# Products that nobody reads in TensorE's waits, and three first-pass products moved into the last projection

## The chip, the cores and the metric

One core of a Trainium2 chip runs the whole program in one launch. The metric is device time in microseconds (us), as a median over runs. TensorE multiplies matrices, VectorE (DVE) and ScalarE (ACT) work on rows of elements, GpSimd (POOL) does the same more slowly, and SyncE (SP) issues the transfers to and from memory. TensorE has two clock levels, 1.2 and 2.4 GHz; the profile lists which share of the full one was granted.

## The reference, cut to what matters

A half-weighted feed-forward layer with eight gated experts, an attention layer and the same feed-forward layer again, each on a layer-normalised input and added to x. x has 4 x 1024 rows of 128 elements.

```python
x = x + 0.5 * _L0_ffn_ref(_layernorm(x), ...)
x = x + _L0_attn_ref(_layernorm(x), ...)
x = x + 0.5 * _L0_ffn_ref(_layernorm(x), ...)
...
# attention: 16 query heads of 8 elements, 4 key/value heads
q = (qkv @ Wq + bq).reshape(B, S, H, dh).transpose(0, 2, 1, 3)
...
scores = jnp.einsum('bhgqd,bhkd->bhgqk', qg, k) * scale
bias = slopes.reshape(KVH, G, 1, 1) * rel
bias = jnp.where(causal, bias, -jnp.inf)
attn = jax.nn.softmax(scores + bias[None], axis=-1)
out = jnp.einsum('bhgqk,bhkd->bhgqd', attn, v)
```

## The kernel before, in words

The 4096 rows are cut into 8 groups of 512 (`GROUPS`, index `c`). The first feed-forward layer is done for all groups; its last stage, `ffn_down`, does for each group the down products (`down`), and on the way the layer norm, the transposition (`xn_T`) and the projections to queries, keys and values for attention (`project`). A projection is one product for the queries (`wq`, 512 columns), four for the values and four for the keys. ACT takes queries and keys out of PSUM (`qk`: `qp`, `qf`, then `kp`, `kf`), DVE and POOL split them into three bfloat16 parts, SP stores the parts to memory (`store_parts`) and loads them back in the layout that attention reads (`load_stack`).

Attention runs over 16 units (a batch entry and a key head). It has two passes. The first finds the maximum of each query's scores: TensorE makes 38 products per unit (`piece`, numbered by `n`), and DVE reduces each one from PSUM (`reduce`). The products of the next unit are made while the second pass of the current one runs (`score`, the exponential on ACT, `times_v`). A ring of three PSUM banks (`RING`) holds the first-pass products: product n can be made only when the one three places before it in the ring has been reduced. The second pass needs the maxima as rows beside the queries; DVE computes them (`maxima`), TensorE transposes them (`maxima_T`), DVE copies them out (`rows_out`, tile `wt`), and SP transfers them (`load_maxima`).

Unit 0 has no unit before it. Its first-pass products start inside `ffn_down`: products 0 to 18 are spread over groups 4 to 7 by `EARLY`, six more (19 to 24, `TAIL`) stand around the transposition of group 7, ahead of its projection, and the last 13 stand at the start of attention. Everything is ordered by hand: each engine runs its list in the written order, and a wait holds up all that stands behind it on that engine.

Three lists matter here.

- TensorE: products 12 and 13, transposition of group 6, products 14 and 15, projection of group 6, products 16 to 18, `maxima_T(0, 0)`, products 19 to 21, transposition of group 7, products 22 to 24, projection of group 7, products 25 to 37, then `score`.
- DVE: reductions 19 to 24, `values(7)` (takes the values of group 7 out of PSUM; it waits until ACT has written `kf`), reductions 25 to 27, `middle(7)` (the second part of group 7's queries, placed by `LAST_SPLIT`), reductions 28 to 37, `maxima(0, 1)`.
- SP: `load_maxima(0, 0, 0)`, `store_parts(7)` (waits until POOL has made the last parts, which wait for `middle(7)`), a wait until all stores have landed, then `load_maxima(0, 0, 1)`. `score` of step 4 of unit 0 waits for that last load (`a_wd[1]`).

Of the kernel before, what the change touches and what calls it, by code (L numbers as in the profile page):

```python
# [2 lines left out]

# [14 lines left out]
GROUPS = TILES // GT  # L18
# [91 lines left out]

EARLY_END = sum(map(sum, EARLY))
TAIL = (3, 3)
LAST_SPLIT = EARLY_END + sum(TAIL) + 3
assert FIRST_HALF <= early(GROUPS - 1, 1).start and LAST_SPLIT < NP1
W1_STEP = 0
# [14 lines left out]
def after(eng, sem, value):  # L131

    if value > 0:
        eng.wait_ge(sem, value)
# [42 lines left out]
def macaron(nc, dram, out):  # L177
    ctx = ExitStack()
    with ctx:
# [17 lines left out]
        c128 = sb("c128", [P, 8 * P])  # L197
# [135 lines left out]
        def bank(b):  # L333
            return ps[:, b, :]
# [723 lines left out]
        def _(pe):  # L1058
            def mm(o, l, r, start=True, stop=True):
                return pe.matmul(o, l, r, start=start, stop=stop, skip_group_check=True)  # L1060
# [59 lines left out]
                    up(k)  # L1120

            def ffn_down(f, qkv):
                def early_pieces(some):
                    for n in some:
                        if n == 0:
                            pe.wait_ge(a_ld[0][0], 16 * LOADS)
                            pe.wait_ge(s_ks0, 4)
                        if n == SECOND_STACK:
                            pe.wait_ge(a_ld[1][0], 16 * LOADS)
                        piece(0, n)  # L1130

                def down(c, par, transpose=False):
                    pe.wait_ge(f.hm, MASK_PARTS * (c + 1))
                    after(pe, f.x, c - 1)
                    if c == 1:
                        pe.wait_ge(f.h, len(TILE_ORDER))
                    for t in range(GT):
                        if transpose and t == GT // 2:
                            xn_T(c - 2)
                        if transpose and t == GT - 1:  # L1140
                            early_pieces(early(c - 1, 0))
                        rows = slice(t * P, (t + 1) * P)
                        for i in range(HT):
                            ins = mm(ps[:, y_bank(qkv, par), rows], h_all[:, c, i, rows], wds[:, i, :],
                                     start=(i == 0), stop=(i == HT - 1))
                    ins.then_inc(f.Y, 1)

                def project(c, par):
                    pe.wait_ge(f.xTb, c + 1)
                    after(pe, f.qf, c)  # L1150
                    mm(bank(5), wq[:, :], xnT[:, par, :]).then_inc(f.Q, 1)
                    w = KVH * DH
                    after(pe, f.v, c)
                    for t in range(GT):
                        ins = mm(ps[:, 4, w * t:w * t + w], xnT[:, par, t * P:(t + 1) * P], wkv[:, w:2 * w])
                    ins.then_inc(f.V, 1)
                    after(pe, f.kf, c)
                    for t in range(GT):
                        ins = mm(ps[w * t:w * t + w, 4, P:2 * P], wkv[:, 0:w], xnT[:, par, t * P:(t + 1) * P])
                    ins.then_inc(f.K, 1)  # L1160

                def xn_T(c):
                    pe.wait_ge(f.xn2, c + 1)
                    after(pe, f.xTb, c)
                    turn(lambda t: xn[:, t, :], 3).then_inc(f.Tb, 1)

                def body(c, par, first, last):
                    if not last:
                        down(c + 1, 1 - par, qkv and not first)
                    if qkv and last:  # L1170
                        xn_T(c - 1)
                        early_pieces(early(c, 0))
                    if qkv and not first:
                        project(c - 1, 1 - par)
                        early_pieces(early(c, 1))

                pe.wait_ge(f.wds, 1)
                down(0, 0)
                over_groups(body)
                if qkv:  # L1180
                    maxima_T(0, 0)
                    early_pieces(range(EARLY_END, EARLY_END + TAIL[0]))
                    xn_T(GROUPS - 1)
                    early_pieces(range(EARLY_END + TAIL[0], EARLY_END + sum(TAIL)))
                    project(GROUPS - 1, 1)

            ring = Ring()

# [69 lines left out]
            def attention():  # L1258
                def next_stack(i, par, half):

                    pe.wait_ge(a_ld[half][1 - par], 8 * LOADS * (i + 3 if par else i + 2))

                pe.wait_ge(a_ld[1][0], 16 * LOADS)
                for n in range(EARLY_END + sum(TAIL), NP1):
                    piece(0, n)
                pe.wait_ge(a_wd[0], 32)
                for p in range(SLOTS):
                    score(0, 0, p, 0)

                def body(i, par, first, last):  # L1270
                    def pieces(s, k):
                        for n in () if last else part(s, k):
                            if n == 0:
                                next_stack(i, par, 0)
                            if n == SECOND_STACK:
                                next_stack(i, par, 1)
                            piece(i + 1, n)

                    for s in range(NSTEP):
                        pieces(s, 0)  # L1280
                        if s + 1 == QT:
                            pe.wait_ge(a_wd[1], 32 * (i + 1))
                        if s + 1 == NSTEP and not last:
                            pe.wait_ge(a_wd[0], 32 * (i + 2))
                        for p in range(SLOTS):
                            if s + 1 < NSTEP:
                                score(i, s + 1, p, par)
                            elif not last:
                                score(i + 1, 0, p, 1 - par)
                            pieces(s, 1 + p)  # L1290
                        if s >= LAG:
                            times_v(i, s - LAG, par)
                        elif not first:
                            times_v(i - 1, NSTEP + s - LAG, 1 - par)
                        pieces(s, 3)
                        if s == W1_STEP:
                            maxima_T(i, 1)
                        if s == OT1_STEP and not first:
                            out_T(i - 1, 1)
                        if s == OT0_STEP:  # L1300
                            out_T(i, 0)
                        if s == W0_STEP and not last:
                            maxima_T(i + 1, 0)

                over_units(body)
                for s in range(NSTEP - LAG, NSTEP):
                    times_v(UNITS - 1, s, 1)
                out_T(UNITS - 1, 1)
# [92 lines left out]
```

## Time and profile before

| | us |
|---|---|
| median of 3 runs (lowest to highest) | 728.12 (727.83 to 728.29) |
| the profiled execution's own time | 728.65 |
| its span, first to last instruction | 726.8 |
| mean granted TensorE clock | 0.977 |

| engine | busy us | share of the span |
|---|---|---|
| TensorE products (PE) | 699.3 | 96% |
| TensorE weight loads (PEld) | 364.1 | 50% |
| DVE | 567.9 | 78% |
| ACT | 406.6 | 56% |
| POOL | 139.6 | 19% |

The page cuts the span into 40 slices of 18.2 us and gives the busy share of each engine in tenths, and the granted clock. The chain that ended last is the work that set the end, followed back from the last instruction; TensorE has 59% of it and DVE 16%. Most of the span is attention, whose 16 units repeat a period of 25.7 us. The change is at its head, between about 148 and 186 us.

### The profile page before, as it was taken

The page shows a single profiled execution, that of the slowest core. Times are in us where ns is not written, and L with a number is a line of the kernel's source. Part 1 is how long each engine was busy: PE and PEld are TensorE (multiplying, and loading weights), DVE is VectorE, ACT ScalarE, POOL GpSimd, SP SyncE. Part 2 cuts the span into 40 slices and gives each one's busy share as a digit, 9 for nine tenths or more (in the row PEclk, how much of TensorE's full clock was granted, in tenths as well). Part 3 has the DMA queues.
Part 4 walks back from the last instruction along what each step waited for, and adds up shares of the span by engine and source line. Part 5 has one row for each costly group of instructions (what it writes and reads, how often), then busy time and mean ns, then how long its engine had stood idle before and what let it go on. Part 6 is the DMA issues. An engine that isn't in the chain of part 4 may idle for free.

```text
span 726.8 us, 15935 instructions
## 1 busy us (share of the span) xinstructions
PE 699.3 (96%) x5906; PEld 364.1 (50%) x5906; DVE 567.9 (78%) x1880; ACT 406.6 (56%) x587; POOL 139.6 (19%) x157
## 2 busy tenths in 40 slices
PE   8999999979999999999999999999999789999998
PEld 4554498833344444444444444444444265544597
DVE  6976338697999999999999999999999148775311
ACT  3353353224776777777777677777767843353200
POOL 3202895552000000000000000000000002104950
PEclk9999999965999999999999999999999999999999
DMA  8014533443001001100100110010010000005651
GB/s 221 1 17 75 92 70 115 142 150 105 21 21 39 21 22 38 39 21 21 39 21 21 39 31 25 24 39 21 21 40 1 2 1 1 1 1 100 107 87 59
DMA packets 47249, 34.69 MB, mean 48 GB/s; under 512 B 13106, under 2 KB 46514, under 8 KB 47172
## 3 DMA queue, kind: packets, MB, share of 16 engines
q1 hardware_dynamic: 46596, 33.60, 19.3%
q8 instruction: 47, 0.77, 0.5%
q14 instruction: 30, 0.25, 0.1%
q10 hardware_dynamic: 576, 0.08, 0.1%
HBM read 23.01 MB, written 10.39 MB: 46 GB/s over the span
## 4 chain that ended last, share of the span: by engine, by line
PE 59%; DVE 16%; issue 13%; DMA 4%; SPq 3%; POOL 3%; ACT 2%; DVEq 0%; ACTq 0%; POOLq 0%
PE ps L1060 55%; DVE mx L945 8%; PE ps L1065 4%; POOL h_all L495 2%; DMA mask_second<-sel_scr 2%; DVE mx L938 1%; ACT h_all L653 1%; DMA yT<-sel_scr 1%; DVE xn L734 1%; DMA k_scr<-kp 1%; SPq L392 1%; DVE stats L722 1%; DVE h_all L938 1%; SPq L389 1%; DVE wb L965 1%
## 5 line engine op out<-in xcount | busy, mean ns | idle before, releaser
L653 ACT ACTIVATE h_all<-ps 128x1024 f32<-128x1024 f32 (+3 forms) x384 | 291.3, 810 | 108.3 <-PE ps L1060 105.2
L945 DVE TENSOR_REDUCE mx<-ps 128x1 f32<-128x512 f32 (+2 forms) x352 | 223.0, 681 | 9.5 <-PE ps L1060 6.5
L1060 PE MATMUL ps<-ks,xnT_all 57*128 57x512 bf16 (+3 forms) x768 | 178.0, 337 | 10.5 <-DVE mx L938 4.7
L1060 PE MATMUL ps<-h_all,vb 128*32 128x512 f32 (+3 forms) x1536 | 163.9, 500 | 0.6 <-ACT osb L642 0.6
L1060 PE MATMUL ps<-xnT_all,ks 59*128 59x512 bf16 (+3 forms) x768 | 158.6, 332 | 3.3 <-ACT h_all L653 3.2
L938 DVE CUSTOM_DVE_ANT_0 h_all<-ps,mask_w 128x384 bf16<-128x384 f32 (+1 forms) x256 | 149.2, 618 | 4.1 <-issue 2.4
L1060 PEld LDWEIGHTS ps<-ks,xnT_all 57*128 57x128 bf16 x768 | 56.3, 94 | 137.7 <-DVE mx L938 63.3
L1060 PE MATMUL ps<-cb 64*128 64x64 bf16 (+3 forms) x1216 | 112.5, 215 | 0.0
L746 DVE TENSOR_TENSOR h_all<-ps,sg 128x512 f32<-128x512 f32 x80 | 55.2, 690 | 50.0 <-PE ps L1060 48.3
L581 ACT ACTIVATE sg<-ps 128x512 f32<-128x512 f32 x80 | 47.8, 597 | 82.6 <-PE ps L1060 82.3
L1060 PEld LDWEIGHTS ps<-cb 64*128 64x128 bf16 x1216 | 80.1, 96 | 17.0 <-issue 0.4
L1060 PE MATMUL ps<-xnT_all,wg 128*128 128x512 f32 x160 | 83.3, 602 | 0.0
L1060 PE MATMUL ps<-xnT_all,wu 128*128 128x512 f32 x160 | 81.7, 592 | 0.0
L1060 PE MATMUL ps<-wds,h_all 128*128 128x128 f32 x640 | 74.9, 276 | 0.0
L1060 PEld LDWEIGHTS ps<-wds,h_all 128*128 128x128 f32 x640 | 72.8, 192 | 2.8 <-issue 2.6
L538 POOL COPY vb<-v_all 128x64 f32<-128x64 f32 x16 | 3.7, 238 | 356.1 <-PE ps L1060 356.1
L1060 PEld LDWEIGHTS ps<-xnT_all,ks 59*128 59x128 bf16 x768 | 45.0, 93 | 42.6 <-ACT h_all L653 26.2
L1060 PEld LDWEIGHTS ps<-h_all,vb 128*32 128x32 f32 x1536 | 30.6, 108 | 38.1 <-issue 29.1
L1060 PEld LDWEIGHTS ps<-xnT_all,wu 128*128 128x128 f32 x160 | 30.4, 190 | 38.3 <-issue 38.0
L482 POOL TENSOR_TENSOR rstd<-ve,mhalf 128x4 f32<-128x4 f32 x24 | 24.2, 1010 | 113.6 <-DVE ve L728 113.5
L1060 PEld LDWEIGHTS ps<-xnT_all,wg 128*128 128x128 f32 x160 | 28.9, 190 | 28.7 <-issue 28.7
L495 POOL TENSOR_TENSOR h_all<-h_all,attn 128x512 f32<-128x512 f32 x24 | 27.1, 1166 | 67.7 <-DVE h_all L746 35.5
(128 smaller groups left out, 552.8 us busy)
## 6 DMA issues: line engine op xcount, KB each, us to landing
xnT_all<-q_scr SPq DMA_DIRECT2D x64, 96.0 KB
attn<-sel_scr SPq DMA_DIRECT2D x12, 256.0 KB, 6.8
mask_second<-sel_scr SPq DMA_DIRECT2D x12, 256.0 KB, 7.7
q_scr<-qp SPq DMA_DIRECT2D x8, 384.0 KB
ks<-k_scr SPq DMA_DIRECT2D x64, 48.0 KB
x<-in_x SPq DMA_DIRECT2D x8, 256.0 KB, 5.9
yT<-sel_scr SPq DMA_DIRECT2D x8, 256.0 KB, 9.0
q_scr<-qp SPq DMA_DIRECT2D x8, 256.0 KB
```

What stands on the lines that cost most here:

```text
L389: sp.dma_start(q_scr[b, :, r:r + products, n], qp[:, par, part, None, :].broadcast_to([P, products, GN])).then_inc(dw, 16)
L392: sp.dma_start(k_scr[b, :, r + m, n].rearrange("k (t n) -> t k n", t=GT), kp[:, par, m])\
L482: pool.tensor_tensor(rstd[:, par, :], ve[:, par, :], mhalf[:, :], ALU.pow).then_inc(rs_sem, 1)
L495: pool.tensor_tensor(h_all[:, c, tiles, :], h_all[:, c, tiles, :], expert_mask[b][:, tiles, :], ALU.mult).then_inc(f.hm, 1)
L581: act.activation(sg[:, b, :], bank(3 + b), ACT.Silu).then_inc(f.sg, 1)
L653: act.activation(pr[:, (NSTEP * i + s) % PR_BUFS, p:HPG:SLOTS, lo:HALF], ps[:, b:b + 2, lo:HALF], ACT.Exp)\
L722: ins = dve.bn_stats(stats[:, par, t, :], x[:, c * GT + t, :])
L746: dve.tensor_tensor(h_all[:, TILE_ORDER[k][0], TILE_ORDER[k][1], :], bank(5 + b), sg[:, b, :], V.mult)\
L938: dve.tensor_tensor_reduce(out=junk, in0=ps[:, b, 0:w], in1=mask_w[:, HALF - w:HALF], scale=1.0, scalar=LOWEST, op0=V.add, op1=V.max, accu ...
L945: dve.tensor_reduce(m, src, AX.X, V.max).then_inc(a_out, 1)
L1060: return pe.matmul(o, l, r, start=start, stop=stop, skip_group_check=True)
L1065: ins = pe.transpose(ps[:, b, t * P:(t + 1) * P], src(t), ident)
```

## The change

`fill(cols)` is a product of a 128x128 tile of ones with the first `cols` columns of a constant tile (`c128`), both in four-byte floats, into PSUM bank 7, which nobody reads from. One of 512 columns stands ahead of the transposition of group 6 (behind a wait until group 6's down products have been taken out of bank 7); one of 256 columns stands behind each of products 14 to 24; one of 128 columns stands behind each of products 28 to 37. Products 25, 26 and 27 move from the start of attention into the projection of group 7: behind the query product, the value products and the key products. With `TAIL` three longer, DVE's lists follow.

```diff
-TAIL = (3, 3)
+TAIL = (3, 3, 3)
+FILL = 256
 LAST_SPLIT = EARLY_END + sum(TAIL) + 3
...
-                def early_pieces(some):
+                def early_pieces(some, filled=False):
...
                         piece(0, n)
+                        if filled:
+                            fill(FILL)
...
-                def project(c, par):
+                def project(c, par, between=()):
+                    some = iter(between)
...
                     mm(bank(5), wq[:, :], xnT[:, par, :]).then_inc(f.Q, 1)
+                    early_pieces(itertools.islice(some, 1))
...
                     ins.then_inc(f.V, 1)
+                    early_pieces(itertools.islice(some, 1))
...
                     ins.then_inc(f.K, 1)
+                    early_pieces(some)
...
                     if qkv and last:
+                        pe.wait_ge(f.x, c)
+                        fill(2 * FILL)
                         xn_T(c - 1)
-                        early_pieces(early(c, 0))
+                        early_pieces(early(c, 0), True)
                     if qkv and not first:
                         project(c - 1, 1 - par)
-                        early_pieces(early(c, 1))
+                        early_pieces(early(c, 1), last)
...
-                    early_pieces(range(EARLY_END, EARLY_END + TAIL[0]))
+                    early_pieces(range(EARLY_END, EARLY_END + TAIL[0]), True)
                     xn_T(GROUPS - 1)
-                    early_pieces(range(EARLY_END + TAIL[0], EARLY_END + sum(TAIL)))
-                    project(GROUPS - 1, 1)
+                    early_pieces(range(EARLY_END + TAIL[0], EARLY_END + sum(TAIL[:2])), True)
+                    project(GROUPS - 1, 1, range(EARLY_END + sum(TAIL[:2]), EARLY_END + sum(TAIL)))
+
+            def fill(cols):
+
+                mm(ps[:, 7, 0:cols], ones[:, :], c128[:, 0:cols])
...
                 for n in range(EARLY_END + sum(TAIL), NP1):
                     piece(0, n)
+                    fill(FILL // 2)
```

TensorE from the transposition of group 7 to the start of attention, before (`ks,xnT_all` is a first-pass product, `c,xn` the transposition, `xnT,wq`, `wkv,xnT` and `xnT,wkv` the projection's queries, values and keys, `c,ones` a product that nobody reads):

```order
L1065 MATMUL ps<-c,xn 128x128 x3
L1060 MATMUL ps<-ks,xnT_all 128x384 [waits a_out] x3
L1060 MATMUL ps<-xnT,wq 128x512 [waits f1_qf,f1_xTb]
L1060 MATMUL ps<-wkv,xnT 128x32 [waits f1_v]
L1060 MATMUL ps<-wkv,xnT 128x32 x3
L1060 MATMUL ps<-xnT,wkv 32x128 [waits f1_kf]
L1060 MATMUL ps<-xnT,wkv 32x128 x3
L1060 MATMUL ps<-ks,xnT_all 128x384 [waits a_out,a_ld_second_even]
```

The same place now, from the last of the three products ahead of the projection:

```order
L1062 MATMUL ps<-ks,xnT_all 128x384 [waits a_out]
L1062 MATMUL ps<-c,ones 128x256
L1062 MATMUL ps<-xnT,wq 128x512 [waits f1_qf,f1_xTb]
L1062 MATMUL ps<-ks,xnT_all 128x384 [waits a_out]
L1062 MATMUL ps<-wkv,xnT 128x32 [waits f1_v]
L1062 MATMUL ps<-wkv,xnT 128x32 x3
L1062 MATMUL ps<-ks,xnT_all 128x512 [waits a_out]
L1062 MATMUL ps<-xnT,wkv 32x128 [waits f1_kf]
L1062 MATMUL ps<-xnT,wkv 32x128 x3
L1062 MATMUL ps<-ks,xnT_all 128x512 [waits a_out]
```

Each of the three products ahead of the projection has a product that nobody reads behind it, and products 25 to 27 stand between the projection's parts.

DVE from the last reduction ahead of `values(7)`, before (`ISA h_all,mx` and `TENSOR_REDUCE mx` are reductions, `v_all` is `values(7)`, `qp<-qf,qp` is `middle(7)`):

```order
L938 ISA h_all,mx<-ps,mask_w 128x384
L938 ISA mx 128x1
L892 TENSOR_TENSOR v_all<-ps,bv 128x4x32 [waits f1_kf,f1_V]
L936 MEMSET idle 128x1 [waits a_out,a_in]
L938 ISA h_all,mx<-ps,mask_w 128x384
L938 ISA mx 128x1
L945 TENSOR_REDUCE mx<-ps 128x1 [waits a_in] x2
L866 TENSOR_TENSOR qp<-qf,qp 128x512 [waits f1_qf]
```

DVE now:

```order
L940 ISA h_all,mx<-ps,mask_w 128x384
L940 ISA mx 128x1
L947 TENSOR_REDUCE mx<-ps 128x1 [waits a_in] x2
L894 TENSOR_TENSOR v_all<-ps,bv 128x4x32 [waits f1_kf,f1_V]
L947 TENSOR_REDUCE mx<-ps 128x1 [waits a_in] x2
L938 MEMSET idle 128x1 [waits a_out,a_in]
L940 ISA h_all,mx<-ps,mask_w 128x512
L940 ISA mx 128x1
L868 TENSOR_TENSOR qp<-qf,qp 128x512 [waits f1_qf]
```

`values(7)` stands behind reductions 25 to 27 now, and `middle(7)` behind reductions 28 to 30 too. The lists of ACT, POOL and SP are as before.

## Rows read from the trace of the kernel before

**Rows 1.** The page's second part: granted clock in 40 slices, tenths

```profile
PEclk9999999965999999999999999999999999999999
```

**Rows 2.** Stretches: start:end, length, busy us (count) by engine, PEclk, DMA share, GB/s

```profile
148.00:151.00 3.00, 1.31 (x9) 0.57 (x6) 2.97 (x5) 0.87 (x3) 2.92 (x5) 1.00 0.58 171
151.00:152.00 1.00, 0.19 (x1) 0.00 (x0) 0.96 (x2) 0.00 (x0) 0.85 (x1) 0.59 0.15 37
...
574.00:578.00 4.00, 2.51 (x24) 0.60 (x22) 0.48 (x2) 3.81 (x6) 0.00 (x0) 1.00 0.00 0
588.00:591.00 3.00, 1.54 (x12) 1.07 (x11) 1.74 (x5) 0.85 (x2) 0.00 (x0) 1.00 0.00 0
...
185.00:186.00 1.00, 1.00 (x18) 0.63 (x16) 0.31 (x2) 0.10 (x1) 0.00 (x0) 0.84 0.00 0
```

**Rows 3.** Two longer stretches, in the same columns

```profile
145.80:165.50 19.70, 14.44 (x72) 7.68 (x71) 19.14 (x52) 4.91 (x10) 9.76 (x12) 0.64 0.51 155
178.50:185.70 7.20, 7.20 (x60) 2.77 (x58) 5.28 (x25) 4.08 (x7) 0.00 (x0) 0.53 0.04 9
```

**Rows 4.** Timeline of PE: start, us, instruction, [idle before <- releaser]

```profile
150.80 0.39 PE L1060 MATMUL ps<-ks,xnT_all 57*128 57x512 bf16 x1 [0.99 <-DVE mx L945]
152.75 0.61 PE L1060 MATMUL ps<-ks,xnT_all 57*128 57x512 bf16 x1 [1.56 <-DVE mx L945]
...
157.42 0.62 PE L1060 MATMUL ps<-ks,xnT_all 57*128 57x256 bf16 x4
...
160.47 0.29 PE L1217 MATMUL ps<-cb,wb 128*32 128x128 bf16 x1 [1.70 <-DVE mx L945]
161.07 1.33 PE L1060 MATMUL ps<-ks,xnT_all 57*128 57x512 bf16 x3 [0.31 <-DVE mx L945]
...
164.13 2.08 PE L1060 MATMUL ps<-xnT,wq 128*128 128x512 f32 x2
166.00 1.75 PE L1060 MATMUL ps<-wkv,xnT 128*128 128x32 f32 x8
...
168.27 0.92 PE L1060 MATMUL ps<-ks,xnT_all 57*128 57x384 bf16 x3
...
185.26 0.61 PE L1060 MATMUL ps<-xnT_all,ks 59*128 59x512 bf16 x2
```

**Rows 5.** Timeline of PE at the program's start: three 512-column products, twice

```profile
2.03 5.49 PE L1060 MATMUL ps<-vb,ones 128*128 128x512 f32 x6 [2.03 <-POOL vb L472]
...
8.66 2.74 PE L1060 MATMUL ps<-vb,ones 128*128 128x512 f32 x6
```

**Rows 6.** Timeline of DVE

```profile
161.71 1.89 DVE L945 TENSOR_REDUCE mx<-ps 128x1 f32<-128x512 f32 x3
...
169.14 0.29 DVE L892 TENSOR_TENSOR v_all<-ps,bv 128x128 f32<-128x128 f32 x1 [3.68 <-ACT kf L627]
...
171.03 0.68 DVE L866 TENSOR_TENSOR qp<-qf,qp 128x512 bf16<-128x512 f32 x1
...
177.82 0.17 DVE L962 TENSOR_TENSOR mm_<-mx 128x16 f32<-128x16 f32 x1
...
185.69 0.69 DVE L938 CUSTOM_DVE_ANT_0 h_all<-ps,mask_w 128x512 bf16<-128x512 f32 x1 [1.04 <-issue]
```

**Rows 7.** Timeline of ACT: group 7's keys, the second copy

```profile
168.67 0.36 ACT L627 ACTIVATE kf<-ps,bk 128x128 f32<-128x128 f32 x1
```

**Rows 8.** Timeline of POOL: the last part of group 7's queries

```profile
171.79 1.15 POOL L514 TENSOR_TENSOR qp<-sg,qp 128x512 bf16<-128x512 f32 x1 [1.36 <-DVE qp L866]
```

**Rows 9.** Timeline of SP: last store of group 7, the load behind it

```profile
177.38 0.51 SPq L392 DMA_DIRECT2D k_scr<-kp  x1
180.54 1.36 SPq L414 DMA_DIRECT2D xnT_all<-wt  x2
```

**Rows 10.** Stretches of 0.1 us with the last packets of stores and load

```profile
179.90:180.00 0.10, 0.10 (x3) 0.06 (x1) 0.10 (x1) 0.05 (x2) 0.00 (x0) 0.50 0.06 21
182.60:182.70 0.10, 0.10 (x2) 0.00 (x0) 0.10 (x1) 0.00 (x0) 0.00 (x0) 0.50 0.12 23
```

More of the change, by code:

```diff
@@ L1 @@
+import itertools
 from collections import namedtuple
```

## The prediction

> **What bounds the kernel now.** I read the granted clock first. It is full in all slices but two [rows 1], and the stretches of a microsecond place the loss: TensorE was busy for 1.31 us of the three from 148.0 and for 0.19 of the next one, in which the clock fell to its lower level, 1.2 GHz [rows 2]. It came back only in the microsecond from 185 [rows 2]. So some 34 us, the end of the feed-forward layer and the head of attention, run at half the clock, and nothing else does.
>
> What that costs isn't 17 us, because TensorE doesn't set the pace in all of it. Read the two longer stretches next. From 145.8 to 165.5 DVE is busy for 19.14 of 19.70 us [rows 3]: its list of reductions, layer norm and splitting runs without a gap, and TensorE's waits there all end on a reduction (0.99, 1.56 and 1.70 us) [rows 4]. A faster clock brings nothing in that stretch. Then the roles change. DVE stands for 3.68 us until ACT has written group 7's keys [rows 6, 7], which wait for a projection at half clock, 164.13 to 168.27 [rows 4]. And from 178.5 to 185.7 TensorE is busy throughout while DVE has work for 5.28 of 7.20 us [rows 3]. These two places, 3.68 and 1.92 us of DVE's idle time, are what the clock costs: 5.6 us at most. From 185.26, where the scores of step 4 begin [rows 4], the clock is full again and attention goes on in its period, so what the head gains up to that point is what the kernel gains, apart from a few tenths.
>
> **What a product that nobody reads costs.** The program's start has the same kind of product, ones against 512 columns of four-byte floats: three take 5.49 us at half clock and 2.74 us at full clock [rows 5], 1.83 and 0.91 us each (the start's rows show the level by their length). So 256 columns cost 0.46 us at full clock and 0.92 at half, 128 columns 0.23 and 0.46. I take these rows as they stand, with their small tail.
>
> **Does the clock stay?** In the four us from 148.0 TensorE was busy for 1.31 + 0.19 = 1.50 us [rows 2]. The change puts the 512 columns ahead of the transposition and 256 behind product 14 there, 0.91 + 0.46 us, so 2.87 busy of four, and 256 more behind product 15. The clock survived emptier stretches elsewhere: 2.51 us of four from 574, 1.54 of three from 588 [rows 2]. I take it that it survives here. The next wait is worse. With full clock the projection of group 6 is over 1.8 us earlier than 157.42 [rows 4], products 16 to 18 and their three fillers (some 2.1 us) end near 157.8, and the transposition of the maxima can't start before 160.47, since the reduction that it waits for comes from DVE [rows 4]. That leaves 2.6 us with nothing to do, more than in the wait of 1.70 us now. I come back to it with the rivals.
>
> **The sum, with the clock kept.** (a) From 161.07, where DVE releases product 19, to the query product of group 7 at 164.13 TensorE needed 3.06 us [rows 4]. At full clock half of that, 1.53, and six fillers of 0.46, 2.74 in all: the query product starts at 165.34, 1.2 us later than now. The fillers are not free here: each delays what stands behind it. (b) Then the projection: 0.91 for the queries, 0.22 for product 25, half of the 2.27 us from 166.00 to 168.27 [rows 4] for values and keys, 0.22 for product 26. The keys are done at 167.8 instead of 168.27, and `kf` at 168.6 instead of 169.03 [rows 7]. (c) DVE now uses its wait: reductions 25 to 27 (0.5, 0.63, 0.63, the latter from 1.89 for three [rows 6]) run as the products arrive, the last, made at 167.8 and ready 0.4 later, until 168.9; `values(7)` ends at 169.2. Before, DVE had the same work behind it at 171.03 [rows 6]. Gain 1.8 us, and the first pass of unit 0 ends 1.8 us before 177.82 [rows 6]. The fillers of 128 columns behind products 28 to 37 add 0.23 to 0.22 us, less than the 0.63 us of a reduction, and hide behind DVE. (d) The last stage: DVE needed 7.87 us from 177.82 to 185.69, of which 1.92 were idle [rows 3, 6]. At full clock it is at that reduction at 176.0 + 5.95 = 182.0, and TensorE, whose work there halves, is no later.
>
> So DVE and TensorE would give 3.7 us. But another chain comes last. The scores of step 4 need the load behind group 7's stores. That chain starts with `middle(7)` on DVE, 171.03; POOL follows at 171.79 [rows 8], the last store is issued at 177.38 and the load at 180.54 [rows 9], when the stores' last packets have been in since 180.0 [rows 10]. The load's last packet comes at 182.7 [rows 10]; with the same 0.5 us from packet to release, TensorE may go on at 183.2. Now the load hides: TensorE arrives at 185.26. The change moves `middle(7)` behind three more reductions, 1.9 us, so it starts at 169.2 + 1.9 = 171.1: no earlier than now. **The gain ends at 185.26 - 183.2 = 2.06 us.** In the profiled execution that is 728.65 - 2.06 = 726.6. This execution lies 0.53 us over the median of 728.12, against which I predict 726.1.
>
> The bounds of (a): if fillers fell only into waits, products would follow DVE, `middle(7)` could start at 161.71 + 1.89 + 1.5 for 22 to 24 + 1.75 + 0.25 + 1.9 = 169.0, and the load would come 2.0 us earlier: the gain is then the 3.7 us of (d), 724.4. At the other end all 2.74 us stay in the way, as I took them. I take the latter, because the waits left between 161.07 and 164.13 are a few tenths (0.31 in [rows 4]).
>
> The order of the rows speaks for that as well: the transposition at 160.47 waits, and all products behind it come later [rows 4]. The Trainium skill, "TensorE: Matmul & The Clock Gate" (Part 2, step 1), says that matmuls stay in program order and only weight loads are pulled ahead. By this rule a released product can't pass a filler, and the sum is 726.1; if products could pass, it would be the 724.4 of the bound. The trace agrees with the rule.
>
> **Rivals.**
>
> *The clock falls in the 2.6 us wait after all.* For: it fell after stretches with 1.31 of 3 and 0.19 of 1 us busy [rows 2], and from 157.8 to 161.07 there is only one small product. Against: the stretch on both sides is full now. From 161.07 on fillers and products are back to back; at the start such products ran 5.49 us until the clock had risen [rows 5]. So up to 5.5 us run at half clock, and TensorE loses half of it, 0 to 2.75 us, all of it ahead of the keys, and so of `middle(7)` and the load. With 1.6 us lost the gain is 0.5: 727.6. The skill's same page (Part 1, "What's actually happening") says that the gate's beat doesn't start with the kernel and that the transition moves from run to run; by this rule some executions would keep the clock, 726.1, and others not, 727.6. One trace can't show it. Chance 0.29.
>
> *Slower: the clock falls there and stays down to the end of the first pass, as it does now.* Then the fillers are what TensorE waits for. 3.06 + 6 x 0.92 = 8.6 us from 161.07 put the query product at 169.7; 4.14 us of projection and two products of 0.43 put the keys at 174.6 and `values(7)` to 175.6. Products 28 to 30 cost 0.43 + 0.46 each, more than a reduction: `middle(7)` at 178.3, 7.2 us late, the load at 190.4, and the kernel at 728.1 + 5.2 = 733.3. For: it took until 185 to come back last time. Against: what ran then were mostly narrow products and waits; fillers are the kind that raised it at the start. It decides from 4.1 us at half clock behind 161.07 (2.06 lost), and is measurable from 7.0 us. With every length between, chance 0.16.
>
> *The fillers cost nothing* (the bound): 724.4, chance 0.05.
>
> *The clock is kept but DVE sets the pace and nothing comes of it*: speaks against it that DVE stands idle for 3.68 us for the projection alone [rows 6]. Inside the first rival's time, no chance of its own.
>
> **How the numbers follow.** The forecast has 0.50. The measurement can tell about 0.2%, 1.46 us, from no change: faster means below 726.7. The forecast and the free fillers lie below it nearly whole, and a little of the first rival: 0.45 + 0.05 + 0.03 = 0.53. Within: the rest of the forecast, most of the first rival, and the mild part of the slower case: 0.05 + 0.25 + 0.01 = 0.31. Slower by over 0.2%: 0.16, with the first rival's worst end. The range leaves out the free fillers' extreme and the slower case beyond about 3 us lost: 724.7 to 729.6.
>
> **What would show it.** Right: granted clock 1.00 from 148 to 186; the wait of 3.68 us ahead of `values(7)` under 1 us; `middle(7)` at about 171; TensorE's scores of step 4 waiting for the load, at about 183.2, with DVE idle ahead of them. Wrong: a clock of 0.5 in the microseconds behind 160; a query product of group 7 later than 166; `middle(7)` later than 172; or scores of step 4 that wait for something else.

## The result, and the profile after

The changed kernel is slower: its median is 731.33 us (20 runs, 727.82 to 741.79) against 727.00 us (20 runs, 724.40 to 731.38), a ratio of 1.0064 with an interval of 1.0045 to 1.0082. The forecast was 726.1 us, in a range of 724.7 to 729.6. The profiled execution took 729.91 us (span 728.1, mean granted clock 0.993).

One thing has to be known to read all that follows. Executions of one and the same program differ in how long TensorE ran at the lower level of its clock, and the mean granted clock tells how long: a mean of 0.993 over 728 us is some 10 us at half clock, 0.977 some 33 us. The changed kernel's runs go from 0.997 (727.82 us) over 0.992 (732.54) to 0.976 (739.51). The kernel before runs at 0.988 to 0.972, so with more half-clock time than the changed kernel's better runs, and yet its median is the lower one. **In its better runs the change gives most of the clock back, and it still loses time.** The ratios below leave out runs more than 1.5% above the fastest of their kernel (three of the changed kernel, four of e2, one each of e3 and e4 at a mean clock of 0.748, which the column "clock" leaves out too, and one of the kernel before, 3578.99 us); the medians don't.

The stretches of after, in the columns of [rows 2], with the page's row of the granted clock ahead of them:

```profile
PEclk9999999989999999999999999999999999999999
```

```profile
148.00:151.00 3.00, 3.00 (x15) 1.36 (x11) 2.93 (x7) 0.97 (x3) 2.92 (x5) 1.00 0.56 168
151.00:152.00 1.00, 1.00 (x4) 0.69 (x5) 0.96 (x4) 0.00 (x0) 0.95 (x1) 1.00 0.13 29
157.00:158.00 1.00, 0.15 (x1) 0.00 (x0) 1.00 (x3) 0.00 (x0) 0.33 (x1) 1.00 0.46 129
158.00:159.00 1.00, 0.23 (x1) 0.09 (x1) 1.00 (x3) 0.00 (x0) 0.82 (x1) 1.00 0.33 96
159.00:160.00 1.00, 0.96 (x3) 0.50 (x3) 1.00 (x3) 0.00 (x0) 0.00 (x0) 0.74 0.54 151
160.00:166.00 6.00, 6.00 (x15) 2.68 (x13) 2.25 (x6) 0.60 (x1) 0.00 (x0) 0.50 0.62 183
166.00:167.00 1.00, 1.00 (x4) 0.40 (x3) 0.37 (x2) 0.00 (x0) 0.00 (x0) 0.85 0.51 126
167.00:186.00 19.00, 17.84 (x138) 8.92 (x139) 15.87 (x59) 8.30 (x14) 5.12 (x8) 1.00 0.21 64
```

The first place is filled: TensorE is busy for 3.00 us of the three from 148.0 (1.31 before, [rows 2]) and the clock stays. Then it is nearly idle for two microseconds (0.15 and 0.23 busy), the clock falls in the microsecond from 159, and the stretch behind it is where the roles change: TensorE is busy for 6.00 of 6.00 us at half clock, and DVE for 2.25. Before, DVE was the busy one there [rows 3].

TensorE's timeline of after shows what it was busy with (`c,ones` is a product that nobody reads; to be held against [rows 4]):

```profile
156.45 0.70 PE L1062 MATMUL ps<-c,ones 128*128 128x256 f32 x2
158.44 0.23 PE L1231 MATMUL ps<-cb,wb 128*32 128x128 bf16 x1 [1.30 <-DVE mx L947]
159.04 0.39 PE L1062 MATMUL ps<-ks,xnT_all 57*128 57x512 bf16 x1 [0.37 <-DVE mx L947]
...
160.43 0.60 PE L1062 MATMUL ps<-ks,xnT_all 57*128 57x512 bf16 x1
160.96 1.22 PE L1062 MATMUL ps<-c,ones 128*128 128x256 f32 x2
162.11 0.60 PE L1062 MATMUL ps<-ks,xnT_all 57*128 57x512 bf16 x1
...
167.94 1.02 PE L1062 MATMUL ps<-xnT,wq 128*128 128x512 f32 x2
...
185.51 0.39 PE L1062 MATMUL ps<-xnT_all,ks 59*128 59x512 bf16 x2
```

From product 19 (159.04) to the query product of group 7 (167.94) TensorE needs 8.90 us; it needed 3.06 [rows 4]. At half clock a first-pass product takes 0.53 us (160.43 to 160.96) and the filler behind it 1.15 (160.96 to 162.11). DVE, SP and the weight loads of TensorE (PEld) show who waits for it:

```profile
165.19 0.55 DVE L940 CUSTOM_DVE_ANT_0 h_all<-ps,mask_w 128x384 bf16<-128x384 f32 x1 [1.75 <-issue]
...
171.88 0.28 DVE L894 TENSOR_TENSOR v_all<-ps,bv 128x128 f32<-128x128 f32 x1
173.89 0.69 DVE L868 TENSOR_TENSOR qp<-qf,qp 128x512 bf16<-128x512 f32 x1
```

```profile
180.25 0.51 SPq L394 DMA_DIRECT2D k_scr<-kp  x1
182.95 1.36 SPq L416 DMA_DIRECT2D xnT_all<-wt  x2
```

```profile
185.51 0.10 PEld L1062 LDWEIGHTS ps<-xnT_all,ks 59*128 59x128 bf16 x2 [0.29 <-DMA xnT_all<-wt]
```

`values(7)` is at 171.88 and `middle(7)` at 173.89 (169.14 and 171.03 before, [rows 6]); the last store of group 7 follows at 180.25, the load of the maxima at 182.95 ([rows 9]: 177.38 and 180.54), and the scores of step 4 wait for that load until 185.51.

These times hide part of the loss, since this execution reached the place some 2 us earlier than the one of before, through a piece of DVE's list that the change does not touch (last section). So the table below counts from product 19.

Behind 185.5 the untouched end of the kernel cost 1.1 us more than before, 728.1 - 185.51 = 542.6 us against 726.8 - 185.26 = 541.5, and one row of the output projection shows why:

```profile
589.00:593.00 4.00, 3.38 (x15) 3.15 (x16) 1.29 (x4) 1.19 (x2) 0.00 (x0) 0.57 0.00 0
```

There the clock fell too. It had stayed up at that place in the execution of before [rows 2].

### The profile page after: what moved, and what is told of

Same layout as the page of the kernel before. It is cut to its first block, busy times and chain, and to the rows that moved or that the text cites. A ratio compares the mean times of both kernels' runs of the same rounds, so it can differ in the third digit from the quotient of the medians.

```text
span 728.1 us, 16023 instructions
## 1 busy us (share of the span) xinstructions
PE 704.0 (97%) x5950; PEld 369.5 (51%) x5950; DVE 566.7 (78%) x1880; ACT 406.4 (56%) x587; POOL 139.3 (19%) x157
## 4 chain that ended last, share of the span: by engine, by line
PE 60%; DVE 15%; issue 13%; POOL 4%; DMA 3%; SPq 3%; ACT 2%; DVEq 0%; ACTq 0%; POOLq 0%
PE ps L1062 55%; DVE mx L947 8%; PE ps L1067 4%; POOL h_all L497 3%; DMA mask_second<-sel_scr 2%; ACT h_all L655 2%; DVE mx L940 1%; DMA k_scr<-kp 1%; SPq L394 1%; DVE xn L736 1%; DVE stats L724 1%; DVE h_all L940 1%; SPq L391 1%; DVE mv L728 0%; DVE wb L967 0%
## 5 line engine op out<-in xcount | busy, mean ns | idle before, releaser
L1062 PE MATMUL ps<-ks,xnT_all 57*128 57x512 bf16 (+3 forms) x768 | 174.2, 328 | 6.7 <-DVE mx L940 3.9
L1062 PE MATMUL ps<-xnT_all,ks 59*128 59x512 bf16 (+3 forms) x768 | 156.5, 329 | 4.3 <-ACT h_all L655 4.1
L1062 PE MATMUL ps<-cb 64*128 64x64 bf16 (+3 forms) x1216 | 110.4, 212 | 0.0
L1062 PEld LDWEIGHTS ps<-cb 64*128 64x128 bf16 x1216 | 78.6, 95 | 16.3
```

## The experiments

Three theories stood at the start. **A:** the clock falls in the wait ahead of `maxima_T(0, 0)`, and the fillers behind it then stand in the way at half clock. **B:** the move costs, by the later `middle(7)`. **C:** the fillers cost more than their columns at full clock too. Ratios are to the kernel before, from the runs on the same chip. The table gives, from the profiled execution of each kernel, the distance in us from the start of product 19 to the query product of group 7, to `middle(7)`, to the issue of the load, and to the scores of step 4; "clock" is the lowest and the highest mean granted clock of its runs (6 to 12 of each kernel from e1 on). The distances are of one execution each: for e2 (741.47 us) and e12 (726.77) it is one of the longest, for e8 (729.98) the shortest.

| kernel | median us | ratio (interval) | clock | query | middle(7) | load | step 4 |
|---|---|---|---|---|---|---|---|
| before | 727.0 | 1 | 0.972-0.988 | 3.06 | 9.96 | 19.47 | 24.19 |
| after | 731.33 | 1.0064 (1.0045-1.0082) | 0.976-0.997 | 8.90 | 14.85 | 23.91 | 26.47 |
| e1, move only | 728.32 | 1.0001 (0.998-1.0022) | 0.974-0.979 | 3.05 | 11.71 | 20.61 | 23.76 |
| e2, fillers only | 734.63 | 1.0077 (1.0051-1.0102) | 0.974-0.995 | 8.87 | 16.52 | 33.25 | 36.50 |
| e3, fillers to 18 | 726.78 | 0.9996 (0.9977-1.0015) | 0.979-0.985 | 3.06 | 11.72 | 20.68 | 24.07 |
| e8, none behind 28-37 | 733.43 | 1.0084 (1.0053-1.0115) | 0.975-0.986 | 8.95 | 14.90 | 24.08 | 27.31 |
| e9, none behind 19-24 | 732.22 | 1.0065 (1.0041-1.0088) | 0.976-0.991 | 2.95 | 12.14 | 25.08 | 28.40 |
| e4, as e3, wait filled | 724.33 | 0.9959 (0.9938-0.9979) | 0.988-0.993 | 2.77 | 8.83 | 18.03 | 21.25 |
| e11, the same again | 724.14 | 0.9975 (0.9948-1.0003) | 0.977-0.993 | 2.78 | 8.83 | 17.98 | 20.52 |
| e10, all, wait filled | 726.99 | 0.9992 (0.9973-1.0011) | 0.995-0.999 | 5.87 | 11.82 | 20.77 | 24.17 |
| e5, e4 + 28-37 | 724.73 | 0.9971 (0.9955-0.9986) | 0.993-0.998 | 2.78 | 8.83 | 17.76 | 20.32 |
| e6, e5 in bfloat16 | 724.72 | 0.9975 (0.9954-0.9997) | 0.981-0.995 | 2.78 | 8.83 | 18.07 | 20.87 |
| e7, e6, middle(7) early | 726.17 | 0.9991 (0.997-1.0012) | 0.978-0.993 | 2.78 | 7.02 | 18.43 | 21.75 |
| e12, e4 without the move | 724.79 | 0.9968 (0.9944-0.9993) | 0.986-0.993 | 2.78 | 7.76 | 17.22 | 22.00 |

### Each half of the change alone: e1 and e2

e1 keeps the move and takes all fillers out:

```diff
-                        pe.wait_ge(f.x, c)
-                        fill(2 * FILL)
...
-                    early_pieces(range(EARLY_END, EARLY_END + TAIL[0]), True)
+                    early_pieces(range(EARLY_END, EARLY_END + TAIL[0]))
...
-                    fill(FILL // 2)
```

> The three products stay inside the projection of group 7 and middle(7) behind reduction 30, but no product that nobody reads is left. Theory A (the clock still falls in the wait ahead of the maxima's transposition, and from then on the fillers themselves are what TensorE's useful products wait for): without fillers the loss is gone, and the moved products fill part of DVE's 3.7 us wait: ratio 0.996 to 1.000 to the kernel before, granted clock about 0.977 as before. Theory B (the moved products cost: they make the keys later, and middle(7), the stores and the load of the maxima with them): slower, 1.003 to 1.006, with or without fillers. Theory C (fillers cost their time at full clock too): as A here.

Its ratio is 1.0001 (0.998 to 1.0022): the move by itself is worth nothing either way, and B falls. The profiled execution has the half clock of before (one stretch shown, columns as above), and `middle(7)` 1.75 us later behind product 19 brings the scores of step 4 no later (23.76 us against 24.19).

```profile
152.00:182.00 30.00, 25.84 (x136) 11.50 (x138) 25.15 (x85) 10.96 (x18) 9.68 (x15) 0.50 0.41 122
```

e2 is the other half, fillers without the move:

```diff
-TAIL = (3, 3, 3)
+TAIL = (3, 3)
```

> All fillers stay, and products 25 to 27 and middle(7) stand where they stood before. Theory A: at least as slow as the change, 1.006 to 1.010, with a time that rises with the share of half clock from execution to execution. Theory B: about the kernel before, 0.999 to 1.002. Theory C: 1.006 to 1.010, but the same in every execution, whatever its clock.

The ratio is 1.0077 (1.0051 to 1.0102). The loss is the fillers'. The profiled execution of e2 is one of its longest (741.47 us), and for 25 us TensorE is busy throughout at half clock:

```profile
161.00:186.00 25.00, 25.00 (x68) 12.69 (x67) 10.66 (x34) 3.77 (x6) 5.11 (x8) 0.50 0.29 87
```

### Which fillers: e3, e8, e9

e3 keeps the fillers up to product 18, and the move. e8 is the changed kernel without the ten fillers behind 28 to 37; e9 is the changed kernel without the six behind 19 to 24.

```diff
-                    early_pieces(range(EARLY_END, EARLY_END + TAIL[0]), True)
+                    early_pieces(range(EARLY_END, EARLY_END + TAIL[0]))
...
-                    early_pieces(range(EARLY_END + TAIL[0], EARLY_END + sum(TAIL[:2])), True)
+                    early_pieces(range(EARLY_END + TAIL[0], EARLY_END + sum(TAIL[:2])))
```

(e9: these lines; e8: only `fill(FILL // 2)` goes; e3: both.)

> The change without the fillers behind products 19 to 24 and 28 to 37; those up to product 18 stay, where DVE sets the pace. Theory A: the fillers that are left cost nothing, the clock falls near 160 all the same: 0.995 to 1.000. Theory B: 1.003 to 1.006. Theory C: fillers in the stretch that DVE sets are free in C as well: 0.996 to 1.001.

> The change without the fillers of 128 columns behind products 28 to 37 alone. Theory C: 1.2 us less than the change when the clock is kept, and more when it isn't: 1.002 to 1.005. Theory A: where the clock is back by 167, as in the change's profile, nothing is saved by it and the clock may fall again in the waits between products: 1.003 to 1.007. The fillers behind 14 to 24 stay, so the fall near 160 does too.

> The changed kernel without its fillers behind products 19 to 24; those behind 14 to 18 and behind 28 to 37 stay, and nothing fills the wait ahead of the transposition of the maxima. If the fillers behind 19 to 24 are what the change pays for (six that stand between DVE's releases and the keys), the time comes back to that of the kernel before, 0.998 to 1.001, although the clock still falls near 159. If the fillers behind 28 to 37 carry the loss, it stays near 1.005. If the fall of the clock alone carries it, whatever stands behind, it stays near 1.005 too, and the clock list must then be like the changed kernel's.

e3 gives 0.9996, e8 1.0084, e9 1.0065. So the price is not the sum of two prices: either sort alone costs as much as both. The first of e9's cases, that the six behind 19 to 24 are what the change pays for, is out; and e8's ratio lies above both of its ranges, which ended at 1.005 and 1.007, though its interval reaches into the second. The traces say how that can be. In e9 the clock falls behind the same wait (0.70 in the microsecond from 162) and stays down until 186; the stretch, and three steps of TensorE's and one of DVE's timeline in it:

```profile
163.00:186.00 23.00, 22.90 (x94) 10.92 (x93) 13.64 (x44) 6.71 (x10) 5.11 (x8) 0.50 0.32 93
```

```profile
171.00 0.79 PE L1062 MATMUL ps<-c,ones 128*128 128x128 f32 x2
171.72 0.60 PE L1062 MATMUL ps<-ks,xnT_all 57*128 57x512 bf16 x1
172.26 0.79 PE L1062 MATMUL ps<-c,ones 128*128 128x128 f32 x2
```

```profile
174.90 0.69 DVE L940 CUSTOM_DVE_ANT_0 h_all<-ps,mask_w 128x512 bf16<-128x512 f32 x1 [0.57 <-issue]
```

A product and its 128-column filler take 172.26 - 171.00 = 1.26 us there, twice the 0.62 that DVE needs for a reduction, so the first pass goes at TensorE's pace and DVE waits about 0.57 us ahead of each. That is the second half of the prediction's slower rival, in a kernel with ten of its fillers. In e8 it is the other way about: the six fillers run at half clock (8.95 us to the query product), the clock returns at 166, and without the later fillers it falls a second time.

```profile
166.00:167.00 1.00, 1.00 (x4) 0.39 (x3) 0.20 (x2) 0.00 (x0) 0.00 (x0) 0.83 0.31 93
...
173.00:174.00 1.00, 0.87 (x2) 0.18 (x2) 1.00 (x3) 0.08 (x1) 0.17 (x1) 0.58 0.00 0
174.00:186.00 12.00, 11.34 (x78) 4.56 (x77) 10.89 (x43) 5.30 (x8) 2.72 (x4) 0.50 0.27 83
```

Once the clock has fallen, the fillers that happen to run then are paid at nearly twice the price (256 columns at 1.15 us in after, at 0.63 in e10 below), whichever they are.

### Keeping the clock there: e4, e10, e11

e4 is e3 with two fillers of 512 columns in the wait itself; e11 is e4 once more; e10 has the same two lines in the full change.

```diff
                 if qkv:
+                    fill(2 * FILL)
+                    fill(2 * FILL)
                     maxima_T(0, 0)
```

> As the run with fillers up to product 18 alone, and two more of 512 columns ahead of the transposition of the maxima, 1.7 to 1.9 us at full clock, into the wait of 1.3 us in which the clock fell in the changed kernel's profile. Theory A: the clock no longer falls there; if it then holds up to attention, the projection of group 7 runs at full clock and the gain is 2 us or a little more, 0.995 to 0.998; if it falls later, between 161 and 175, where TensorE waits for DVE again, 0.997 to 1.001. Theory B: 1.003 to 1.006.

> The changed kernel with all its fillers, and two fillers of 512 columns in the wait ahead of the transposition of the maxima, so that the clock should be kept through 159. If the fall of the clock in that wait is the whole of the loss, this is my forecast's case: the query product some 4.3 us behind product 19, and a ratio near 0.997. If the fillers behind 19 to 24 cost more than their columns at full clock too, the query product comes 5 us or more behind product 19 and the ratio is 1.000 to 1.004, with a mean clock of 0.993 or more.

> The kernel of e4_wait_filled once more, beside the other two on the same chip: fillers up to product 18, two of 512 columns in the wait ahead of the transposition of the maxima, none behind 19 to 24 and 28 to 37. If its gain was that of the kernel and not of one chip's draws, the ratio is 0.995 to 0.998 again. Against e10_all_and_wait it differs by the fillers behind 19 to 24 and 28 to 37 alone: 2 to 5 us if those stand on the path at either clock, under 1 us if they are free once the clock is kept.

These bear A out. With the two lines the full change comes from 731.33 to 726.99 us (ratio 1.0064 to 0.9992), and its runs have clocks of 0.995 to 0.999. The wait is what the fall hangs on; the fall itself shows behind it, where TensorE is at work again (in e2 only in the microsecond from 161, after 2 us of work without a gap). The kernel without the fillers behind 19 to 24 and 28 to 37 comes from 726.78 (e3) to 724.33 and 724.14. e4 beats both kernels, with the lowest ratio of all that ran; the repetition has nearly the same median, with an interval that just reaches 1.0003 (one of its runs took 733.83 us at a mean clock of 0.977). TensorE's timeline of e11, from the filler of product 18 on:

```profile
156.46 2.42 PE L1062 MATMUL ps<-c,ones 128*128 128x256 f32 x6
158.81 0.23 PE L1233 MATMUL ps<-cb,wb 128*32 128x128 bf16 x1
159.03 0.39 PE L1062 MATMUL ps<-ks,xnT_all 57*128 57x512 bf16 x1
159.63 0.51 PE L1062 MATMUL ps<-ks,xnT_all 57*128 57x512 bf16 x2 [0.21 <-DVE mx L947]
...
161.55 0.33 PE L1062 MATMUL ps<-ks,xnT_all 57*128 57x384 bf16 x1 [0.27 <-DVE mx L947]
161.81 1.13 PE L1062 MATMUL ps<-xnT,wq 128*128 128x512 f32 x2
...
179.55 0.39 PE L1062 MATMUL ps<-xnT_all,ks 59*128 59x512 bf16 x2 [0.31 <-DMA xnT_all<-wt]
```

The idle 1.30 us of after are gone, product 19 starts when it did, and the scores of step 4 come 20.52 us behind it, not 26.47.

e10 shows C as well, with the clock at 1.00 up to 180 us (one stretch, and the timeline from product 19):

```profile
157.00:180.00 23.00, 21.95 (x136) 11.21 (x134) 18.52 (x58) 7.87 (x12) 6.38 (x10) 1.00 0.42 124
```

```profile
159.24 0.39 PE L1062 MATMUL ps<-ks,xnT_all 57*128 57x512 bf16 x1
159.56 0.70 PE L1062 MATMUL ps<-c,ones 128*128 128x256 f32 x2
160.19 0.39 PE L1062 MATMUL ps<-ks,xnT_all 57*128 57x512 bf16 x1
...
162.52 0.33 PE L1062 MATMUL ps<-ks,xnT_all 57*128 57x384 bf16 x1
162.78 0.70 PE L1062 MATMUL ps<-c,ones 128*128 128x256 f32 x2
...
165.11 1.02 PE L1062 MATMUL ps<-xnT,wq 128*128 128x512 f32 x2
```

A product takes 0.32 us and its filler 0.63, and the query product stands 5.87 us behind product 19 where e11 has 2.78. So the six fillers cost 3.1 us at full clock too, and the medians agree: 726.99 - 724.14 = 2.85 us for all sixteen later fillers (the intervals of the two ratios overlap).

### Fillers at the head of attention: e5, e6, e7

e5 is e4 with the 128-column fillers behind 28 to 37 put back; e6 has bfloat16 fillers of 256 columns in their place; e7 is e6 with `LAST_SPLIT` three smaller, so that `middle(7)` stands ahead of reduction 28.

```diff
                 for n in range(EARLY_END + sum(TAIL), NP1):
                     piece(0, n)
+                    fill(FILL // 2)
```

> The run with the filled wait (0.9959), and the change's fillers of 128 columns behind products 28 to 37 again, none behind 19 to 24. Theory C (a filler costs more than its columns, at any clock): ten times 0.12 = 1.2 us lost, less 0.4 that a clock kept through the head of attention gives back: 0.9965 to 0.998. Theory A (only fillers at half clock cost): the clock, which fell at 166.6 there, is kept, and the head of attention gains: 0.992 to 0.9955.

> As the run before, but the fillers behind products 28 to 37 are two-byte products of 256 columns with a two-byte weight tile: one load of about 0.1 us and 0.107 us of columns. Theory C: product and filler fit into the 0.62 us of a reduction, so nothing is lost; if the clock is kept, the scores of step 4 then wait for the load of the maxima at about 179.8 (180.33 in the filled-wait run): 0.994 to 0.996. Theory A: the same. If the thinner fillers don't keep the clock: 0.996 to 0.998.

> As the run before, with middle(7) ahead of reduction 28 instead of behind reduction 30. Theory of the store chain (middle(7), POOL's last part, the stores, their landing, the load of the maxima, 11.9 to 12.2 us in all, set the scores of step 4 once the clock is kept): middle(7) starts 1.9 us earlier and the scores with it, down to what DVE's reductions need, so 1.0 to 1.9 us faster than the run before: 0.991 to 0.994. Rival (the chain isn't what comes last): as the run before, 0.994 to 0.996.

e5 and e6 give 0.9971 and 0.9975. Against e4 they are neither better nor worse by what these runs can tell. In e5's profiled execution the clock is at 1.00 from 148 to 186, and `middle(7)` and the load come no later than in e4 (8.83 and 17.76 us behind product 19, against 8.83 and 18.03): at full clock the fillers at the head hide behind DVE, and the clock that they keep brings nothing that can be seen in the time. The thinner fillers of e6 don't keep it (0.50 from 168 to 174). e7 missed its expectation: `middle(7)` comes 1.8 us earlier behind product 19 (7.02 against 8.83), the load does not (18.43 against 18.07). SP's and DVE's timelines of e7 say why:

```profile
176.09 0.51 SPq L394 DMA_DIRECT2D k_scr<-kp  x1
180.50 0.66 SPq L416 DMA_DIRECT2D xnT_all<-wt  x1
```

```profile
180.20 0.21 DVE L956 COPY wt<-ps 32x128 bf16<-32x128 bf16 x1
```

From the last store to the load there are 4.4 us, where after has 2.70. The load also needs the rows that it carries, and their copy ended at 180.41, 0.09 us ahead of it. Two chains end at the load, one over the stores, 8.9 to 9.2 us from `middle(7)` wherever it is the later one, and one over the end of the first pass.

### The move with the clock kept: e12

e12 is e4 with `TAIL = (3, 3)`.

> The kernel of e4_wait_filled without its move: products 25 to 27 stand at the start of attention again, and the second part of group 7's queries behind reduction 27. The clock is kept ahead of the projection as in e4_wait_filled. If the move uses DVE's wait for the keys, as my step (c) has it, leaving it out costs 1 to 2 us against e4_wait_filled: a ratio of 0.997 to 0.999. If the move is worth nothing even with the clock kept, as it was without fillers, the ratio is that of e4_wait_filled, 0.994 to 0.997, and the second part of group 7's queries and the load for step 4 come no later than there.

The median is 724.79, 0.5 us above e4's, with intervals that lie over each other (0.9944 to 0.9993 and 0.9938 to 0.9979). Within that it stays open whether the move is worth anything. That the move gives 1 to 2 us isn't borne out; `middle(7)` even comes 1.1 us earlier without it (7.76 against 8.83).

## Why the prediction was wrong, point by point

**What bounds the kernel** held. Up to product 19 DVE is busy throughout and the clock buys nothing (e3, which keeps it to 158, has 0.9996); the 5.6 us that the prediction gave as the most to be had were not reached by any kernel. e4 and e11 have 2.9 us of them by their medians.

**"Does the clock stay?"** is the step that failed first. Its first half held: the fillers behind 14 to 18 kept the clock from 148 to 158. Its second half had the right place, too long a wait (2.6 us up to the transposition of the maxima; the rows have 1.30 us ahead of it and 0.37 behind), and the wrong verdict: the sum counts on the clock, and behind this wait it fell, to 0.50 for 6.8 us. In after against e10, the same kernel with the wait filled, that is worth 731.33 - 726.99 = 4.3 us. All that the prediction had against a fall there was that the stretch is full on both sides; it was, and the clock fell. The rows near 574 and 588, with which it argued for the first half, are no bound either. They were one draw: in this execution of after the clock fell at the second place, in code that the change doesn't touch, and in e11 at the first one (0.50 from 571 to 574), behind the same wait of 1.01 us. A stretch in which the clock happened to stay once is no bound for another. The prediction had the fall as two rivals at 0.29 and 0.16, together below the forecast; with a stretch as empty as the one in which the clock had fallen before (0.19 of a microsecond, [rows 2]), the fall should have been the forecast.

**The slower rival** is what happened, as one end of a spread: e2's long execution shows it whole (half clock from 161 to 191), e9 its second half, and after sits between it and the forecast. Its working has 8.6 us to the query product at half clock, and the trace 8.90, which is partly luck: some 2 us of the 8.90 ran at full clock (up to 159.5 and from 166.3 on), and each filler cost more than the working had (1.15 us against 0.92). That the start's 5.49 us [rows 5] were at half clock is read from their length alone; the granted clock of 2 to 8 us is 1.00 in the profile. What it missed is that the clock may come back, in this execution at 166, and then be kept by the fillers at the head (in e8, without them, it fell again at 173); the median is 731.3 and not 733.3. The Trainium skill, "TensorE: Matmul & The Clock Gate" (Part 1, "What's actually happening"), says that the transition moves from run to run; the mean clocks of 0.976 to 0.997 agree.

**(a) The fillers** were mis-sized, the second step that failed. With the clock kept e10 measures the term by itself: 5.87 us to the query product, not 4.27. TensorE's rows have no wait in them there. The six fillers take 3.61 us of it (0.54 to 0.64 each, up to the start of what follows), not 2.74, and products and transposition 2.26, not 1.53: a product with a filler behind it takes 0.32 us up to the filler's start, or 0.26 with 384 columns, where the prediction has 0.22. Nor would TensorE have been there in 1.53 us without them: e11 needs 2.78 at full clock, since it waits for DVE's reductions (0.21 and 0.27 us in the rows above). So six fillers cost 3.1 us. Between products 128 columns take 0.42 us (168.33 to 168.75 in e10) and 256 take 0.63. At the start of the program three of them follow each other with the same weights [rows 5]; the columns cost nearly what the start says (0.21 against 0.23 for 128), and another 0.21 come with each change from product to filler. The bound "fillers cost nothing" fell as the prediction had it.

**(c)** split in two. That the fillers of 128 columns hide behind DVE is right at full clock, in spite of 0.74 us for product and filler where I had 0.45: `values(7)` and `middle(7)` stand between DVE's reductions, so DVE is behind, and in after it is busy for 1.00 of every microsecond from 171 to 178. At half clock it is wrong (e9). That the move uses DVE's wait is right by the rows, and in the time nothing of it can be seen (e1, e12): what DVE saves there, `middle(7)` gives back by standing three reductions later.

**(d) The chain over the stores** is confirmed as the end of the head in after and e11, where the scores wait 0.29 and 0.31 us for that load, 11.6 and 11.7 us from `middle(7)`; the prediction had 12.1. But in the execution of before it had company. The load at 180.54 [rows 9] stands right behind DVE's copy of the rows that it carries:

```profile
180.19 0.21 DVE L954 COPY wt<-ps 32x128 bf16<-32x128 bf16 x1
```

It ended at 180.40. By the 8.9 to 9.2 us of the other executions the stores alone would have let the load go at 179.9 to 180.2. The two chains were that close, and I followed only one; e7 shows what that costs.

With the clock kept, e10 is the case that the prediction forecast, and 726.99 us against 726.1 look close. That is luck. The forecast came from three runs with a median of 728.12 us, less a gain of 2.06; beside e10 the kernel before has 727.07, so the gain measured is 0.1 us (ratio 0.9992, interval 0.9973 to 1.0011). The scores of step 4 come 24.17 us behind product 19, where the sum has 183.2 - 161.07 = 22.1. Of these 2 us 1.8 are there at `middle(7)` already (11.82 against 10.0), 1.6 of them by term (a); at the end the clock fell again (0.54 in the microsecond from 180), and TensorE reached the scores 3.40 us behind the load's issue, not the 2.56 of after.

## What to carry to other kernels

Work that only keeps the clock has its price in the same place as other work: put it into a wait that the trace shows, at most as long as that wait, and not between a release and what is waited for. Fill the wait behind which the clock falls first; a filler that stands behind it while the clock still falls is paid at half speed, and here ten or six such fillers lost as much as sixteen. Where the clock decides, one execution is one draw: look at the clocks of all runs before a single stretch is taken as evidence.

## What was not expected of the hardware

**TensorE busy throughout does not tell when the clock returns.** In e2 it was busy for 25.00 of 25 us at the lower level, in e9 for 22.90 of 23; in after, with the same kinds of products, the clock came back after 6.8 us. The other way, it fell in e11 in the microsecond from 168, where the row of the microsecond ahead is much like its own:

```profile
167.00:168.00 1.00, 0.56 (x2) 0.09 (x2) 1.00 (x5) 0.00 (x0) 0.00 (x0) 1.00 0.47 119
168.00:169.00 1.00, 0.55 (x1) 0.09 (x1) 1.00 (x3) 0.00 (x0) 0.37 (x1) 0.55 0.59 138
```

**The same DVE operations take twice as long in some executions, where POOL is at work beside them.** The normalisation of group 6, four operations, took 2.03 us in the execution of before and 1.11 in that of after; the changed lines lie behind them. The first two rows are of before, the other two of after.

```profile
147.06 2.03 DVE L734 TENSOR_SCALAR xn<-x,mv,rstd 128x128 f32<-128x128 f32 x4
147.86 1.16 POOL L508 TENSOR_TENSOR sg<-qf,qp 128x512 f32<-128x512 f32 x1 [0.91 <-ACT qf L622]
```

```profile
146.83 1.11 DVE L736 TENSOR_SCALAR xn<-x,mv,rstd 128x128 f32<-128x128 f32 x4
147.96 1.60 POOL L510 TENSOR_TENSOR sg<-qf,qp 128x512 f32<-128x512 f32 x1 [1.24 <-ACT qf L624]
```

In before POOL started 0.8 us into the four operations, in after when they were over. From 115 us on the traces of all fourteen kernels keep to that: 1.10 to 1.12 us with next to nothing of POOL beside the four, 2.03 to 2.49 with POOL at work for more than 1.2 us of them (group 7's took 2.16 in before and 2.49 in after). No run moved POOL's work, so the cause isn't shown. Together with a later step of the maxima (1.10 against 0.19 us) and the second part of a group's queries (0.93 against 0.69) this is the bulk of the 2 us by which product 19 starts earlier in after. It comes without fillers too (e1: product 19 at 159.15) and fails to come in e7 (2.14 us, product 19 at 162.07), where the lists up to there are those of after, so it isn't the change's. e5 and e9 reach product 19 at 160.93 and 160.85 for another reason: they are 1.8 us behind after at 118 already.
